# One core of an audio tower: the causal convolution on the 64-token blocks of one sequence alone, with the band matrices of two tiles packed into one, and a feed-forward whose up products are unsplit float32 and whose gelu output has two buffers

## The chip, the core and the metric

The kernel runs on one core of one Trainium2 chip. Its time is device microseconds (us). The engines are TensorE (PE, with its weight loads as PEld), VectorE (DVE), ScalarE (ACT), GpSimd (POOL) and SyncE (SP), which issues most transfers.

## The reference

Three layers work on 32 sequences of 64 tokens with 1024 features (2048 tokens).

```python
# 1. tokenizer
h = xf @ W_proj + b_proj                        # (32, 64, 1024)
y = _layernorm(h, ln_g, ln_b)
w = softmax((y @ W_wgen + b_wgen).reshape(B, 64, 8, 5), axis=-1)
yp = jnp.pad(y, ((0, 0), (4, 0), (0, 0)))
taps = jnp.stack([yp[:, k:k + 64] for k in range(5)], axis=0).reshape(5, B, 64, 8, 128)
conv = jnp.einsum('kbthr,bthk->bthr', taps, w).reshape(B, 64, 1024)
h = h + relu(conv @ W_ff + b_ff)
# 2. attention with 8 heads of 64 within each sequence
h = h + attn(_layernorm(h), w_qkv, w_o)
# 3. feed-forward of 16 heads, features permuted
t = _layernorm(h)[:, perm].reshape(-1, 16, 64)
t = gelu(jnp.einsum('bhd,hdm->bhm', t, up))     # 64 -> 256 per head
t = jnp.einsum('bhm,hmd->bhd', t, down)         # 256 -> 64 per head
h = h + t.reshape(-1, 1024)[:, unperm]
```

The convolution is causal with 5 taps, and its weights differ for every token and each of 8 heads of 128 features.

## The kernel before

The 2048 tokens are four chunks (`CH`) of `N` = 512, held as 8 blocks of 128 features by 512 tokens. A chunk has `TILES` = 4 tiles of 128 tokens, two sequences each. Every engine's order is written by hand, and counting semaphores are the only sync. The stages follow each other: input projection with the layernorm statistics and the logits (`a_step`, 0 to 211 us); the convolution of chunk 0 (211 to 229); W_ff of chunk c with the convolution of chunk c + 1 beside its last third (`b_step`, to 476); attention (`c_step`, to 808); output projection (`o_group`, to 909); feed-forward (to the end).

Large products are split in three: both operands are cut into a high part (ACT copy to float32r) and a low part (subtraction on DVE or POOL), and `split3` issues high·high, high·low, low·high. The statistics, the transposes, the convolution and the down products are unsplit float32, which the trace shows as two MATMUL records for each call (one for a transpose).

**The convolution as a product with a band matrix.** The softmaxed taps of a tile and head, 128 tokens by 5, are written to DRAM with a skew (`band_skew`) into a buffer that was filled with zeros before (`band_zero`, 2 x 1032 KB for each chunk), and read back as a 128 x 128 band (`band_load`, two transfers of 16 units for each chunk; 32 units are 4 tiles by 8 heads). For head h, `turn(n, h)` transposes the 4 tiles of y and the 4 bands, ACT copies the one (`turn_evac`), DVE the other (`band_evac`), `conv(n, h)` multiplies tile by tile with all 128 tokens contracted, and ACT and DVE make its high and low parts (`conv_high`, `conv_low`) for W_ff. y uses banks 0 and 1, the bands 2 and 3, the result 4 and 5, by turns.

**Weights.** `unit_load` brings units of 128 x 512 through a ring of four `stage` slots; ACT makes the high part (`unit_hi`), DVE or POOL the low one (`unit_lo`, L299), and a slot is loaded again when its low part is done. POOL starts the W_ff units when the last bands of chunk 0 are transposed (`at_mm` of 8). SP's queue has them behind the band loads of chunk 1, and `db_late`, whose mean `late_sum` forms on DVE (L1242) for PE's L319, behind 8 of those units.

**Feed-forward.** A step s is one pair of heads (a = s mod 8) of one chunk, 32 steps in all. `ff_up(s + 1)` fills banks 0 to 3 (two blocks of two row halves, 64 rows contracted; three passes), ACT applies gelu from the banks into `gt` (L1097), `ff_down(s)` multiplies `gt` by `dn_f` into bank 4 or 5 (L1838), DVE adds (`d_add`, L1442), POOL scatters (L763). PE's order is up(s + 1), down(s). Beside it, for the next chunk, POOL gathers (L757), DVE centres and scales (`d_prep`), ACT and DVE split (`xd_high`, `xd_low`). In steps 5 to 12 the variance of the last chunk is formed too: DVE centres a block (L383), ACT squares it (L387), POOL adds it (L341), and PE needs the sum after down(12) (`stat_var_pe`, L403).

## Time and profile before

| | |
|---|---|
| median of 3 runs | 1067.11 us (1065.8 to 1070.73) |
| the profiled execution | 1062.28 us, span 1060.5 us |
| PE, PEld, DVE, ACT, POOL busy | 92%, 70%, 50%, 42%, 38% |
| mean granted TensorE clock | 0.977 |
| DMA packets, MB | 71570, 133.15 |
| chain that ended last | PE 51%, issue 11%, POOL 8%, DVE 5% |
| PE busy in 211 to 275 us | 52.06 of 64.00, clock 0.92 |
| PE busy in 808 to 909.5 us | 88.80 of 101.50, clock 0.92 |
| PE busy in 909.5 to 1060.5 us | 123.4 of 151.0 |

Busy shares say how full an engine's row is; they don't say what a stretch waits for. For that the timeline is read: an engine, its line, what it writes and reads, and in brackets how long it idled before and for whom.

### The profile page before, as it was taken

To read this page: it belongs to the slowest core of one execution; us is meant where nothing else is said; L and a number is where in the kernel's file an instruction comes from. 1 tells how busy PE (TensorE), PEld (TensorE's weight loads), DVE (VectorE), ACT (ScalarE), POOL (GpSimd) and SP (SyncE) were. 2 spreads that over 40 slices of the span, in tenths; PEclk is the share of its full clock that TensorE was granted. 3 is DMA by queue.
4 is the path that set the end of the run, shared out by engine and by line. 5 is a ranking of instruction groups with operands and counts; after the bars stand their busy time and mean duration, and the time that the engine had idled before them with its cause. 6 is when DMAs were issued, how large, how long until landed. Compare 5 with 4: busy or idle time off the path is not lost.

```text
span 1060.5 us, 14600 instructions
## 1 busy us (share of the span) xinstructions
PE 975.1 (92%) x5532; PEld 746.9 (70%) x5532; DVE 534.4 (50%) x848; ACT 443.9 (42%) x757; POOL 400.2 (38%) x321
## 2 busy tenths in 40 slices
PE   7999999987999999999779999999999899788885
PEld 5877777775887988878567877877887677333332
DVE  6253535576457403353756255174064567976661
ACT  6244454544434433434243243242142332676663
POOL 1224343128502114622360450550023577757431
PEclk9999999998999999999989999999999998899999
DMA  8754653595353154327101202001217765634311
GB/s 292 272 199 25 218 39 144 41 339 187 112 172 106 60 149 173 112 96 248 41 11 37 74 11 72 39 12 38 73 58 235 225 218 199 193 115 137 132 60 60
DMA packets 71570, 133.15 MB, mean 126 GB/s; under 512 B 29255, under 2 KB 30279, under 8 KB 66894
## 3 DMA queue, kind: packets, MB, share of 16 engines
q1 hardware_dynamic: 65342, 115.29, 34.7%
q0 software_dynamic: 5120, 16.78, 4.7%
q8 instruction: 44, 0.72, 0.3%
q10 hardware_dynamic: 1040, 0.16, 0.1%
q14 instruction: 24, 0.20, 0.1%
HBM read 85.65 MB, written 46.56 MB: 125 GB/s over the span
## 4 chain that ended last, share of the span: by engine, by line
PE 51%; issue 11%; POOL 8%; DVE 5%; ACT 3%; DMA 3%; SPq 0%; POOLq 0%; ACTq 0%; DVEq 0%
PE bank L305 12%; PE bank L307 12%; PE bank L306 12%; PE bank L1828 4%; POOL vacc L341 3%; PE bank L1838 3%; PE bank L1583 2%; DVE sq L383 1%; ACT gt L1097 1%; DMA stage<-w_qkv_t 1%; POOL hg L757 1%; PE bank L1562 1%; DVE acc L1242 1%; POOL acc L314 1%; PE bank L1570 1%
## 5 line engine op out<-in xcount | busy, mean ns | idle before, releaser
L341 POOL TENSOR_TENSOR vacc<-vacc,sq 128x512 f32<-128x512 f32 x72 | 97.1, 1348 | 47.2 <-ACT sq L387 37.9
L305 PE MATMUL bank<-xa_h,wp_h 128*128 128x512 f32 x256 | 103.0, 402 | 7.2 <-DVE xa_l L1119 7.2
L305 PE MATMUL bank<-cv_h,wf_h 128*128 128x512 f32 x256 | 106.2, 415 | 3.2 <-POOL wf_l L299 3.2
L307 PE MATMUL bank<-cv_h,wf_l 128*128 128x512 f32 x256 | 101.7, 397 | 0.0
L306 PE MATMUL bank<-cv_l,wf_h 128*128 128x512 f32 x256 | 101.6, 397 | 0.0
L306 PE MATMUL bank<-xa_l,wp_h 128*128 128x512 f32 x256 | 100.7, 393 | 0.0
L307 PE MATMUL bank<-xa_h,wp_l 128*128 128x512 f32 x256 | 100.6, 393 | 0.0
L705 POOL TENSOR_TENSOR fo<-fo,res 128x512 f32<-128x512 f32 x32 | 43.7, 1379 | 129.8 <-ACT fo L844 92.8
L1097 ACT ACTIVATE gt<-bank 128x512 f32<-128x512 f32 x128 | 66.0, 601 | 20.2 <-PE bank L1838 20.0
L387 ACT ACTIVATE sq<-sq 128x512 f32<-128x512 f32 x56 | 35.0, 632 | 72.3 <-DVE sq L383 72.3
L1838 PE MATMUL bank<-gt,dn_f 128*64 128x512 f32 x256 | 62.5, 606 | 0.0
L305 PEld LDWEIGHTS bank<-xa_h,wp_h 128*128 128x128 f32 x256 | 48.7, 190 | 18.7 <-DVE xa_l L1119 7.2
L305 PE MATMUL bank<-xc_h,wq_h 128*128 128x512 f32 x128 | 54.7, 427 | 5.5 <-issue 5.5
L305 PEld LDWEIGHTS bank<-cv_h,wf_h 128*128 128x128 f32 x256 | 49.3, 193 | 14.3 <-issue 4.8
L763 POOL DMA_INDIRECT out<-hg,rows x32 | 37.4, 1169 | 54.4 <-DVE hg L1442 52.2
L305 PE MATMUL bank<-vs_h,wo_h 128*128 128x512 f32 x128 | 53.4, 417 | 4.6 <-DVE vs_l L1340 4.2
L307 PEld LDWEIGHTS bank<-cv_h,wf_l 128*128 128x128 f32 x256 | 49.1, 192 | 10.6
L306 PEld LDWEIGHTS bank<-cv_l,wf_h 128*128 128x128 f32 x256 | 49.2, 192 | 10.4 <-issue 1.2
L306 PEld LDWEIGHTS bank<-xa_l,wp_h 128*128 128x128 f32 x256 | 48.7, 190 | 10.6 <-issue 0.7
L307 PEld LDWEIGHTS bank<-xa_h,wp_l 128*128 128x128 f32 x256 | 48.6, 190 | 10.4
L1224 DVE COPY ar<-bank 128x512 f32<-128x512 f32 x32 | 22.1, 689 | 66.7 <-PE bank L1570 66.7
L305 PE MATMUL bank<-wv_h,xc_h 128*128 128x512 f32 x128 | 50.6, 396 | 2.2 <-DVE wv_l L299 2.2
(187 smaller groups left out, 2288.7 us busy)
## 6 DMA issues: line engine op xcount, KB each, us to landing
band_s<-zero SPq DMA_DIRECT2D x8, 1032.0 KB, 9.2
xs<-x_t SPq DMA_DIRECT2D x32, 256.0 KB, 6.3
h_s<-ho SPq DMA_DIRECT2D x8, 1024.0 KB, 6.7
res<-h_s SPq DMA_DIRECT2D x32, 256.0 KB, 3.2
h_s<-fo SPq DMA_DIRECT2D x32, 256.0 KB, 2.3
dc<-h_s SPq DMA_DIRECT2D x4, 2048.0 KB, 9.3
h<-h_s SPq DMA_DIRECT2D x8, 1024.0 KB, 8.4
h_s<-h SPq DMA_DIRECT2D x8, 1024.0 KB, 5.0
```

What stands on the lines that cost most here:

```text
L305: pe.matmul(o, wh, xh, start=start, stop=False)
L306: pe.matmul(o, wh, xl, start=False, stop=False)
L307: return pe.matmul(o, wl, xh, start=False, stop=stop)
L341: g.tensor_tensor(vacc[:, :], t[:, 0, :] if k == 1 else vacc[:, :], t[:, k % 2, :], ALU.add).then_inc(ln_pool, 1)
L387: act.activation(sq[:, k % 2, :], sq[:, k % 2, :], ACT.Square).then_inc(ln_sq, 1)
L705: g.tensor_tensor(fo[m % 4][:, :], fo[m % 4][:, :], res[:, m % 2, :], ALU.add).then_inc(ff_add, 1)
L763: g.indirect_dma_start(out=outs[c], out_offset=bass.IndirectOffsetOnAxis(ap=rows[:, k:k + 1], axis=0), in_=hg[:, hg_block(c) + k, :], in_o ...
L1097: act.activation(gt[:, i, :], bank[i][:, :], ACT.Gelu).then_inc(gelu_ok, 1)
L1224: v.tensor_copy(ar[:, h % 2, :], bank[AT_BANK + h % 2][:, :]).then_inc(ar_ev, 1)
L1583: mm = pe.matmul(bank[CV_BANK + h % 2][:, cols], yt[:, h % 2, cols], ar[:, h % 2, cols], start=True, stop=True)
L1828: mm = pe.matmul(bank[2 * blk + j][:, :], w[r, a, cols], x[r, a, :], start=n == 0, stop=n == len(passes) - 1)
L1838: pe.matmul(bank[4 + a % 2][side, :], dn_f[:, FFB * a + 2 * head + blk, :], gt[:, i, :], start=blk == 0, stop=blk == 1).then_inc(g_used, 1)
```

## The change

The convolution works on each sequence's block of 64 x 64. The band matrix of a unit keeps only 64 rows of the skewed buffer (row pitch 132 instead of 128, so that two sequences' 64 columns lie side by side in 128), and the bands of two tiles fill the two halves of the partitions. A chunk has 16 packed bands instead of 32: half the zeros, half the bytes and rows of `band_load` (in four transfers, not two), two band transposes for each head instead of four, and a copy on DVE of 256 columns, not 512. `conv` is 16 products of 64 x 64 x 64 in the four quarters of the array instead of 4 of 128; its result lies in two banks, one for each sequence of a tile, so `conv_high` and `conv_low` become two instructions of 256 columns each. Only chunk 0 has two pairs of banks; the others have banks 3 and 4 alone, and `conv(n, h)` waits for the low parts of head h - 1. In the feed-forward the up products become one unsplit float32 pass on `dd` and `up_f`; `xd_high`, `xd_low`, and the four units of `up` in the ring go, and `gt` gets a second buffer.

```diff
-BAND = P * (P + 1)
 UNITS = TILES * CONV_HEADS
+ROW = P + TAPS - 1
+BAND = SEQ * (ROW + 1) + SEQ
...
-        up_h = place("up_h", [P, KB, FF_MID], F32R, R1)
-        up_l = place("up_l", [P, KB, FF_MID], F32R, R1 + 8 * KIB)
+        up_f = place("up_f", [P, KB, FF_MID], F32, R1)
-        gt = place("gt", [P, FFB, N], F32, R2)
+        gt = [place(f"gt{i}", [P, FFB, N], F32, at) for i, at in enumerate((R2, R1 + 40 * KIB))]
...
+        def cv_out(n, h, s):
+
+            return bank[cv_banks(n, h)[s]][:, 0:N // 2].rearrange("p (t q) -> p t q", q=SEQ)
...
                 for i in range(2):
-                    part = slice(i * UNITS // 2, (i + 1) * UNITS // 2)
-                    sp.dma_start(dst[:, part, :], src[:, part, :]).then_inc(band_ld[n % 2][i], 16)
+                    part = slice(i * UNITS // 4, (i + 1) * UNITS // 4)
+                    for a in range(2):
+                        sp.dma_start(dst[a * SEQ:(a + 1) * SEQ, part, :], src[a][:, part, :])\
+                          .then_inc(band_ld[n % 2][i], 16)
...
-                act.activation(cv_h[:, h, :], bank[CV_BANK + h % 2][:, :], ACT.Copy).then_inc(cv_hi, 1)
+                for s in range(2):
+                    act.activation(one_seq(cv_h[:, h, :], s), cv_out(n, h, s), ACT.Copy).then_inc(cv_hi, 1)
...
-                    if 8 * c + a > 0:
-                        act.wait_ge(g_used, 4 * (8 * c + a - 1) + i + 1)
-                    act.activation(gt[:, i, :], bank[i][:, :], ACT.Gelu).then_inc(gelu_ok, 1)
+                    if 8 * c + a > 1:
+                        act.wait_ge(g_used, 4 * (8 * c + a - 2) + i + 1)
+                    act.activation(gt[a % 2][:, i, :], bank[i][:, :], ACT.Gelu).then_inc(gelu_ok, 1)
...
             def conv(n, h):
-                if h < 2:
-                    since(pe, ff_ev, n - 1, 8, 5 + h)
-                if h >= 2:
+                if n == 0:
                     since(pe, cv_lo, n, 8, h - 1)
+                elif h == 0:
+                    pe.wait_ge(ff_ev, 8 * (n - 1) + CV_BANKS[0][1] + 1)
+                else:
+                    pe.wait_ge(cv_lo, 8 * n + h)
                 since(pe, yt_ev, n, 8, h + 1)
                 since(pe, ar_ev, n, 8, h + 1)
+                halves = [slice(SEQ * i, SEQ * i + SEQ) for i in range(2)]
                 for t in range(TILES):
-                    cols = slice(t * P, (t + 1) * P)
-                    mm = pe.matmul(bank[CV_BANK + h % 2][:, cols], yt[:, h % 2, cols], ar[:, h % 2, cols],
-                                   start=True, stop=True)
+                    for f in range(2):
+                        col = t * P + f * SEQ
+                        for s in range(2):
+                            mm = pe.matmul(bank[cv_banks(n, h)[s]][halves[f], t * SEQ:(t + 1) * SEQ],
+                                           yt[halves[s], h % 2, col:col + SEQ],
+                                           ar[halves[s], h % 2, t * SEQ:(t + 1) * SEQ], start=True, stop=True)
...
-                passes = ((up_h, xd_h), (up_h, xd_l), (up_l, xd_h))
-                for n, (w, x) in enumerate(passes):
-                    for j, r in enumerate(halves):
-                        mm = pe.matmul(bank[2 * blk + j][:, :], w[r, a, cols], x[r, a, :],
-                                       start=n == 0, stop=n == len(passes) - 1)
+                for j, r in enumerate(halves):
+                    mm = pe.matmul(bank[2 * blk + j][:, :], up_f[r, a, cols], dd[r, a, :], start=True, stop=True)
...
-YT_BANK, AT_BANK, CV_BANK = 0, 2, 4
+YT_BANKS, AT_BANKS, CV_BANKS = (0, 2), (1, 5), ((3, 4), (6, 7))
...
+def cv_banks(n, h):
+
+    return CV_BANKS[h % 2 if n == 0 else 0]
```

On PE, beside the last third of W_ff of chunk 1, one head of chunk 2 stood like this (`db_next` is y, and the last row is the next head's):

```order
L1562 MATMUL bank<-ident,db_next 128x128 x4
L1570 MATMUL bank<-ident,band 128x128 x4
L1583 MATMUL bank<-ar,yt 128x128 x4
L305 MATMUL bank<-cv_h,wf_h 128x512
L306 MATMUL bank<-cv_l,wf_h 128x512
L307 MATMUL bank<-cv_h,wf_l 128x512
```

After the change the same head reads:

```order
L1523 MATMUL bank<-ident,db_next 128x128 x4
L1533 MATMUL bank<-ident,band 128x128 x2
L1551 MATMUL bank<-ar,yt 64x64 x16
L299 MATMUL bank<-cv_h,wf_h 128x512
L300 MATMUL bank<-cv_l,wf_h 128x512
L301 MATMUL bank<-cv_h,wf_l 128x512
```

The order is kept; two transposes are gone and 4 convolution calls became 16 small ones.

On PE at the end of the feed-forward, one step stood as:

```order
L1828 MATMUL bank<-xd_h,up_h 128x512 x2
L1828 MATMUL bank<-xd_l,up_h 128x512 x2
L1828 MATMUL bank<-xd_h,up_l 128x512 x2
L1828 MATMUL bank<-xd_h,up_h 128x512 x2
L1828 MATMUL bank<-xd_l,up_h 128x512 x2
L1828 MATMUL bank<-xd_h,up_l 128x512 x2
L1838 MATMUL bank<-gt,dn_f 64x512 x4
```

And now two steps of it read (the number behind `gt` is the buffer):

```order
L1795 MATMUL bank<-dd,up_f 128x512 x4
L1804 MATMUL bank<-gt_132,dn_f 64x512 x4
L1795 MATMUL bank<-dd,up_f 128x512 x4
L1804 MATMUL bank<-gt_131,dn_f 64x512 x4
L1795 MATMUL bank<-dd,up_f 128x512 x4
```

Twelve up calls became four, and down reads the two buffers by turns.

On SP's queue around the band loads of chunks 0 and 1 (`band_86` is chunk 0's) there stood:

```order
L505 DMA band_86<-band_s 128x16x128 x2
L463 DMA h_s<-ho 128x2048 x2
L474 DMA db_next<-h_s 128x4096
L480 DMA mt<-stat_s 128x512
L481 DMA rt<-stat_s 128x512
L505 DMA band<-band_s 128x16x128 x2
L277 DMA stage<-w_ff 128x512 x8
L474 DMA db_late<-h_s 128x4096
```

and now there stands:

```order
L498 DMA band_86<-band_s 64x8x128 x4
L454 DMA h_s<-ho 128x2048 x2
L465 DMA db_next<-h_s 128x4096
L471 DMA mt<-stat_s 128x512
L472 DMA rt<-stat_s 128x512
L498 DMA band<-band_s 64x8x128 x4
L274 DMA stage<-w_ff 128x512 x8
L465 DMA db_late<-h_s 128x4096
```

The places are the same; each chunk's band load has half the rows.

## Rows read from the trace of the kernel before

**Rows 1.** Timeline of PE, two feed-forward steps: start us, us, engine, line, what, [idle]

```profile
994.67 0.50 PE L1828 MATMUL bank<-xd_h,up_h 64*128 64x512 f32 x2 [0.46 <-ACT gt L1097]
...
998.86 0.50 PE L1828 MATMUL bank<-xd_h,up_h 64*128 64x512 f32 x2 [0.46 <-ACT gt L1097]
...
1000.08 0.39 PE L1828 MATMUL bank<-xd_l,up_h 64*128 64x512 f32 x2
1000.31 0.40 PE L1828 MATMUL bank<-xd_h,up_l 64*128 64x512 f32 x2
1000.64 1.94 PE L1838 MATMUL bank<-gt,dn_f 128*64 128x512 f32 x8
```

**Rows 2.** Timeline of PE, a down group with float32 work right behind it

```profile
918.65 1.94 PE L1838 MATMUL bank<-gt,dn_f 128*64 128x512 f32 x8
920.52 1.12 PE L391 MATMUL bank<-acc,mean_w 128*128 128x512 f32 x2
```

**Rows 3.** Timeline of all engines in one of steps 5 to 12

```profile
961.47 0.50 PE L1828 MATMUL bank<-xd_h,up_h 64*128 64x512 f32 x2 [0.78 <-ACT gt L1097]
...
965.26 0.69 DVE L1442 TENSOR_TENSOR hg<-bank,hg 128x512 f32<-128x512 f32 x1 [1.07 <-PE bank L1838]
...
965.96 0.50 PE L1828 MATMUL bank<-xd_h,up_h 64*128 64x512 f32 x2 [0.78 <-ACT gt L1097]
...
969.24 2.04 ACT L1097 ACTIVATE gt<-bank 128x512 f32<-128x512 f32 x4
969.42 1.26 POOL L341 TENSOR_TENSOR vacc<-vacc,sq 128x512 f32<-128x512 f32 x1 [0.50 <-ACT sq L387]
```

**Rows 4.** Timeline of all engines, one head of chunk 3's convolution beside W_ff

```profile
409.39 0.60 PE L1570 MATMUL bank<-ident,band 128*128 128x128 f32 x4
...
409.82 1.06 PE L1583 MATMUL bank<-ar,yt 128*128 128x128 f32 x8
...
410.64 0.47 PE L305 MATMUL bank<-cv_h,wf_h 128*128 128x512 f32 x1
410.92 0.60 ACT L839 ACTIVATE cv_h<-bank 128x512 fp32r<-128x512 f32 x1 [0.73 <-PE bank L1583]
...
411.55 0.69 DVE L1228 TENSOR_TENSOR cv_l<-bank,cv_h 128x512 fp32r<-128x512 f32 x1 [0.83 <-ACT cv_h L839]
...
412.97 0.50 PE L1583 MATMUL bank<-ar,yt 128*128 128x128 f32 x3
```

**Rows 5.** Timeline of all engines at a product of the attention in 64 x 64 pieces

```profile
807.90 0.69 PE L1735 MATMUL bank<-pt,vv 64*64 64x64 f32 x32
808.52 0.50 PE L305 MATMUL bank<-vs_h,wo_h 128*128 128x512 f32 x1
808.66 0.84 ACT L994 ACTIVATE vo<-bank,vec 128x256 f32<-128x256 f32 x2 [4.65 <-PE bank L1735]
```

**Rows 6.** Timelines of PE, SP, ACT and DVE between 211 and 265 us

```profile
214.17 0.66 PE L1570 MATMUL bank<-ident,band 128*128 128x128 f32 x4 [1.73 <-DMA band<-band_s]
...
218.06 11.55 SPq L505 DMA_DIRECT2D band<-band_s  x2
...
237.39 2.47 ACT L293 ACTIVATE wf_h<-stage 128x512 fp32r<-128x512 f32 x4 [7.86 <-DMA stage<-w_ff]
...
240.23 0.59 PE L305 MATMUL bank<-cv_h,wf_h 128*128 128x512 f32 x1 [3.16 <-POOL wf_l L299]
...
254.38 0.69 DVE L1242 TENSOR_TENSOR acc<-db_late 128x512 f32<-128x512 f32 x1 [8.68 <-DMA db_late<-h_s]
...
264.34 2.08 PE L319 MATMUL bank<-acc,mean_w 128*128 128x512 f32 x2 [5.91 <-DVE acc L1242]
```

**Rows 7.** Windows: PE, PEld, DVE, ACT, POOL busy, clock, DMA share, GB/s

```profile
220.00:225.00 5.00, 5.00 (x48) 5.00 (x47) 3.57 (x6) 3.24 (x6) 0.00 (x0) 1.00 1.04 437
```

**Rows 8.** Timelines of POOL and PE in the output projection

```profile
850.26 6.89 POOL L299 TENSOR_TENSOR up_l<-stage,up_h 128x512 fp32r<-128x512 f32 x4 [3.00 <-ACT up_h L293]
...
875.99 2.00 PE L403 MATMUL bank<-mean_w,vacc 128*128 128x1 f32 x8 [3.03 <-DVE h L1377]
```

More of the change, by code:

```diff
@@ L433, in band_zero @@
                 sp.wait_ge(zero_ok, 1)
-                half = UNITS * BAND // 2
-                for i in range(2):
-                    sp.dma_start(band_s[c, i * half:(i + 1) * half].rearrange("(p n) -> p n", p=P),
-                                 zero[:, :]).then_inc(band_zeroed[c], 16)
+                sp.dma_start(band_s[c].rearrange("(p n) -> p n", p=P), zero[:, :]).then_inc(band_zeroed[c], 16)
             band_zero(0)
@@ L610, in _ @@
                     if c + 1 == CH and m == 0:
-                        for u in range(U_O + 4, U_UP):
+                        for u in range(U_O + 4, U_END):
                             unit_load(sp, u)
@@ L738, in _ @@
             g.wait_ge(v_mm, 4 * CH)
-            for u in range(U_O, U_UP):
+            for u in range(U_O, U_END):
                 unit_lo(g, u)
@@ L775, in _ @@
                 o_sum(c)
-                if c == 1:
-                    for u in range(U_UP, U_END):
-                        unit_lo(g, u)
             gather(1)
@@ L834, in turn_evac @@
                 since(act, cv_mm, n, 8, h - 1)
-                act.activation(yt[:, h % 2, :], bank[YT_BANK + h % 2][:, :], ACT.Copy).then_inc(yt_ev, 1)
+                act.activation(yt[:, h % 2, :], bank[YT_BANKS[h % 2]][:, :], ACT.Copy).then_inc(yt_ev, 1)
             def conv_high(n, h):
                 since(act, cv_mm, n, 8, h + 1)
-                act.activation(cv_h[:, h, :], bank[CV_BANK + h % 2][:, :], ACT.Copy).then_inc(cv_hi, 1)
+                for s in range(2):
+                    act.activation(one_seq(cv_h[:, h, :], s), cv_out(n, h, s), ACT.Copy).then_inc(cv_hi, 1)
             def ff_relu(c, m):
@@ L1047, in c_step @@
                 if not ahead:
-                    for u in range(U_O + 4, U_UP):
+                    for u in range(U_O + 4, U_END):
                         unit_hi(act, u)
@@ L1060, in _ @@
             c_step(CH - 1, False)
-            def xd_high(n, k):
-                since(act, xd_sc, n, 8, k + 1)
-                since(act, up_mm, n - 1, 32, 4 * k + 4)
-                act.activation(xd_h[:, k, :], dd[:, k, :], ACT.Copy).then_inc(xd_hi, 1)
             for c in range(CH):
@@ L1077, in _ @@
                     vs_high(c + 1, range(PAIRS - 1))
-                else:
-                    for half in range(2):
-                        act.wait_ge(o_st[0][half], 16 * (CH // 2))
-                    xd_high(0, 0)
-                    xd_high(0, 1)
                 if c > 0:
@@ L1086, in _ @@
                     vs_high(c + 1, [PAIRS - 1])
-                if c == 1:
-                    for u in range(U_UP, U_END):
-                        unit_hi(act, u)
             def gelus(c, a):
@@ L1173, in gates @@
                 since(v, lgt_mm, n, 1, 1)
-                since(v, skewed, n - 1, 16, 16)
+                since(v, skewed, n - 1, 32, 32)
                 per = [P, UNITS, TAPS]
@@ L1223, in band_evac @@
                 since(v, cv_mm, n, 8, h - 1)
-                v.tensor_copy(ar[:, h % 2, :], bank[AT_BANK + h % 2][:, :]).then_inc(ar_ev, 1)
+                v.tensor_copy(ar[:, h % 2, :], bank[AT_BANKS[h % 2]][:, 0:N // 2]).then_inc(ar_ev, 1)
             def conv_low(n, h):
-                since(v, cv_hi, n, 8, h + 1)
-                v.tensor_tensor(cv_l[:, h, :], bank[CV_BANK + h % 2][:, :],
-                                cv_h[:, h, :].bitcast(F32), ALU.subtract).then_inc(cv_lo, 1)
+                for s in range(2):
+                    v.wait_ge(cv_hi, 16 * n + 2 * h + s + 1)
+                    ins = v.tensor_tensor(one_seq(cv_l[:, h, :], s), cv_out(n, h, s),
+                                          one_seq(cv_h[:, h, :].bitcast(F32), s), ALU.subtract)
+                ins.then_inc(cv_lo, 1)
             for h in range(CONV_HEADS + 1):
@@ L1450, in _ @@
                     d_prep(n + 1, [k])
[L1451 to L1456 removed]
+                d_prep(0, LAST_PREP.get(s, ()))
                 if s == 0:
@@ L1565, in turn @@
                 if h % 4 == 0:
-                    pe.wait_ge(band_ld[n % 2][h // 4], 16 * (n // 2 + 1))
+                    pe.wait_ge(band_ld[n % 2][h // 4], 32 * (n // 2 + 1))
                 if h >= 2:
-                    since(pe, ar_ev, n, 8, h - 1)
-                for t in range(TILES):
-                    mm = pe.transpose(bank[AT_BANK + h % 2][:, t * P:(t + 1) * P], b[:, h * TILES + t, :],
+                    pe.wait_ge(ar_ev, 8 * n + h - 1)
+                elif n > 0:
+                    pe.wait_ge(ff_ev, 8 * (n - 1) + AT_BANKS[h] + 1)
+                for u in range(TILES // 2):
+                    mm = pe.transpose(bank[AT_BANKS[h % 2]][:, u * P:(u + 1) * P], b[:, h * TILES // 2 + u, :],
                                       ident[:, :])
```

92 lines of the change are left out of this document (30 added, 62 removed).

## The prediction, made before the change was run

> **What bounds the kernel now.** I read the page first: PE is busy 92% of the span and holds 51% of the chain, so a stretch can become shorter in two ways, by less PE work where PE is full, or by a shorter wait where it idles. The list of waits says where it idles, and the timeline says why. Three stretches matter.
>
> The feed-forward is a round trip, not a full engine. A step takes 998.86 - 994.67 = 4.19 us, and PE idles 0.46 us in front of each for a gelu [rows 1]. With one `gt`, gelu(s + 1) may overwrite block i only after down(s) has read it, and up(s + 2) needs the bank that gelu(s + 1) empties; the reader is to see that up, down and gelu pass the turn around. In steps 5 to 12 a step takes 965.96 - 961.47 = 4.49 us, since the square stands between two gelu groups on ACT [rows 3].
>
> The convolution beside W_ff is full: a head takes 412.97 - 409.82 = 3.15 us with no idle on PE, and 0.82 us of it is `conv`, 0.43 the four band transposes [rows 4].
>
> Between 211 and 265 us PE waits for transfers and what follows from them: 1.73 us for chunk 0's bands, 3.16 for a W_ff low part, 5.91 for the late mean [rows 6]. The transfer engines are full there [rows 7], and SP holds its queue 11.55 us for chunk 1's two band loads before the first W_ff unit is issued [rows 6].
>
> **The change part by part.**
>
> *Feed-forward, steps without statistics (24).* Up is now four float32 calls of 512 columns in two pairs, where three float32r passes of two blocks stood. Down has four float32 calls of 512 columns in two pairs too; it holds PE from 918.65 to 920.52, 1.87 us, the change of shape behind it included [rows 2]. The trace shows no float32 pair of row halves with 128 columns. From below its cost is that of down, if the two halves overlap as the float32r halves do (both calls of a pass stand in one row of 0.40 us and the passes follow at 0.23 us [rows 1]); from above it is twice that, if they don't. I take 1.87, since the attention's 64 x 64 float32 pieces, which use both row halves, plainly overlap: 16 calls in 0.62 us [rows 5]. PE's work in a step is then 2 x 1.87 = 3.74 us. With two buffers gelu(s + 1) needs only up(s + 1); a gelu group is 2.07 us or less [rows 3] and `xd_high` is gone, so ACT hides in 3.74. DVE loses `xd_low`. The step becomes 3.74, full of PE: 0.45 x 24 = 10.8 us. If this cover were gone (ACT's 2.04 us in line with up, as now), the step would stay at 4.19.
>
> *Steps 5 to 12 (8).* Here the square stays in ACT's order between gelu(s) and gelu(s + 1), and it waits for DVE's centre, behind `d_add` of down(s - 1). From that `d_add` to the next gelu it is 969.24 - 965.26 = 3.98 us [rows 3]; `xd_low` takes 0.6 of it away. PE can now run up and down in the shadow of it in one step, but every second step up waits about 1 us for the late gelu. Worked through, two steps take 8.3 us, 4.15 each. POOL sets a floor: 4.49 - 0.50 idle = 3.99 us [rows 3]. 0.34 x 8 = 2.7 us. The last step's gelu no longer waits for down(30), and the two reloads of ACT's table behind L403 are hidden by two buffers: I take 0.8 us. Feed-forward together: -14.3 us (bounds -20 with no cost for a change of shape and steps 5 to 12 at POOL's floor, 0 if the round trip stays).
>
> *Heads beside W_ff (24).* Two transposes fewer: -0.22 us [rows 4]. `conv` is 0.82 us before. The attention's product has the same 16 calls on the same quarters of the array and takes 808.52 - 807.90 = 0.62 us [rows 5]; I add the 0.10 us that a change of shape costs (down starts 0.33 us behind the last up pass, whose passes follow at 0.23 [rows 1]). So -0.10, and -0.29 for a head with a little lost behind it: -7.0 us. The new wait on `cv_lo` of the head before: ACT begins 0.28 us after the 0.82 of `conv` [rows 4], so 0.90 us after the new start; its two copies take 0.84 [rows 5]; DVE's second half ends by about 2.25 us. The next `conv` comes at 2.86 us. The wait is hidden with 0.6 us to spare; behind it on PE stands the whole of W_ff. Bounds: -0.40 to +0.3 for a head.
>
> At this place the Trainium skill speaks against the change. In "TensorE: Matmul & The Clock Gate", section "Wait — 56ns, not 53.3ns?", it holds that start-to-start never falls below about 25 ns however small the product is. By the page the 32 records would take 0.80 us, `conv` would gain nothing, and the sum would be 3 to 4 us worse. The trace disagrees: 32 records in 0.62 us are 19 ns each [rows 5].
>
> *Chunk 0's convolution and the W_ff ring.* The band transposes of chunk 0 start as soon as y is there: half the rows, so the 1.73 us go. The 8 heads gain 0.3 each (ACT's 0.5 + 0.84 per head still fits in 1.45): -2.4. PE and POOL's first low part are thus some 4 us earlier. SP's band loads of chunk 1 take half of 11.55 us, and the full transfer engines [rows 7] lose half of two chunks' bands, so the first ring unit, landed at 237.39 [rows 6], should land near 229. PE would then need it at 232.7 and find it: the idle of 3.16 us goes, with the slow restart behind it. But what counts is the next wait. `db_late` is loaded behind the ring, and the mean it feeds ends PE's idle of 5.91 us at 264.34 [rows 6]. It moves as the ring moves, and PE arrives earlier too and waits as long as before. I take -9.0 us at that point; bounds 0 (the ring does not move: then all PE gains go into the 5.91) and -10.
>
> *Output projection.* POOL loses 6.89 us of low parts ahead of chunk 2's variance, whose chain ends with PE idle 3.03 us at L403 [rows 8]. At most that can go; I take -2.5. The unsplit `up` loads and fewer zeros cost nothing: they lie in stretches where PE is full.
>
> **The sum.** -14.3 - 7.0 - 9.0 - 2.5 = -32.8 us. The profiled execution took 1062.3 us, so its like would take 1029.5; the median of the runs is 1067.1, 4.8 above it, which would give 1034.3. I put 1032 us.
>
> **The rivals.**
>
> *The round trip stays* (chance 0.12): PE's order or ACT's holds gelu back even with two buffers. For it speaks that steps 5 to 12 keep a chain through DVE. Then no gain of 14.3: 1046 us.
>
> *The single pair of result banks serialises the heads* (0.12): two half copies on each engine have fixed costs, and `conv` waits for `cv_lo`. Against it stand 0.6 us of slack. If it eats the gain: 1039 us; with 0.4 us of wait in each of 21 heads it would be 1047.
>
> *The ring does not move* (0.14): what holds `db_late` is the skewed write or the zeros, which stay in number, and PE's lead goes into the wait for the mean. 1041 us.
>
> *The row halves of unsplit float32 don't overlap* (0.08), the other side. Up takes 2 x 1.72 + 0.15 = 3.6 us, the step 3.6 + 1.87 = 5.5: 24 x 1.3 + 8 x 1.0 = +39 instead of -14.3, so 1032 + 53 = 1085 us. It decides from a step of 4.85 us on, an up group of 3.0: below it the 18.5 us of the other parts keep the kernel faster. Against it stands the 0.62 us of [rows 5].
>
> *As forecast* 0.49; *more than forecast* (both bounds met, under 1015) 0.05.
>
> **How the numbers follow.** The time is the likeliest case's, 1032 (its own range 1020 to 1043). The range takes in the three rivals with less gain, two of them together, and the lower bounds: 1013 to 1053; the serial halves lie outside. A measurement tells about 0.5% from no change here, 5.3 us. Faster by more: 0.89. Within: 0.03, if several rivals meet. Slower: 0.08.
>
> **What would show it.** Feed-forward steps of 3.7 us with no idle before up, near 4.15 in steps 5 to 12; float32 up pairs that start together; heads of 2.86 us; `conv` of 0.62 to 0.72; no idle at the fifth W_ff group; L319 near 255 us. An up group near 3.6 us, or PE idle for `cv_l` in front of `conv`, would make it wrong.

## The result, and the profile after

The changed kernel took 1033.76 us (median of 4 runs, 1031.12 to 1037.73) where the kernel before took 1066.96: the ratio is 0.9686, 95% interval 0.9642 to 0.973. Run again in a later series it took 1032.87 us, ratio 0.9703 (0.9676 to 0.973). The forecast was 1032 us. The sum came out, but two of its four terms did not: the largest was about right, the second largest was a good deal too big, and the smallest was less than half of what came. That the sum came out is in part luck: an error of 7 us at one place met errors the other way at two others (see the account below).

The page of the changed kernel, its profiled execution (1035.96 us, span 1034.2):

```profile
PE 967.4 (94%) x6108; PEld 714.5 (69%) x6108; DVE 509.2 (49%) x848; ACT 424.4 (41%) x753; POOL 394.3 (38%) x317
...
DMA packets 75062, 124.96 MB, mean 121 GB/s; under 512 B 29159, under 2 KB 38375, under 8 KB 70894
...
L1795 PE MATMUL bank<-dd,up_f 64*128 64x512 f32 x256 | 67.9, 651 | 5.6 <-ACT gt L1077 5.4
```

PE lost 7.7 us of work and some 19 us of idle time. The packets rose while the bytes fell; that comes back below.

**Feed-forward.** The timeline of PE, two plain steps, and then all engines in one of steps 5 to 12, as [rows 1, 3]:

```profile
988.83 1.99 PE L1795 MATMUL bank<-dd,up_f 64*128 64x512 f32 x8
990.75 1.94 PE L1804 MATMUL bank<-gt,dn_f 128*64 128x512 f32 x8
992.62 1.99 PE L1795 MATMUL bank<-dd,up_f 64*128 64x512 f32 x8
```

```profile
942.39 2.01 PE L1795 MATMUL bank<-dd,up_f 64*128 64x512 f32 x8
...
944.33 1.94 PE L1804 MATMUL bank<-gt,dn_f 128*64 128x512 f32 x8
944.38 0.68 DVE L377 TENSOR_TENSOR sq<-h,mean_t 128x512 f32<-128x512 f32 x1
945.10 0.63 ACT L381 ACTIVATE sq<-sq 128x512 f32<-128x512 f32 x1 [1.88 <-DVE sq L377]
945.63 2.04 ACT L1077 ACTIVATE gt<-bank 128x512 f32<-128x512 f32 x4
946.85 2.01 PE L1795 MATMUL bank<-dd,up_f 64*128 64x512 f32 x8 [0.58 <-ACT gt L1077]
```

The bracket before up is gone in the plain steps: 1.92 us of up and 1.87 of down make 3.79, no gap between them. In steps 5 to 12 the square still stands between two gelu groups and waits 1.88 us for the centre, and every second up waits.

**A head beside W_ff**, the timeline of PE for chunk 3, as [rows 4]:

```profile
401.06 0.69 PE L1551 MATMUL bank<-ar,yt 64*64 64x64 f32 x32
401.69 0.50 PE L299 MATMUL bank<-cv_h,wf_h 128*128 128x512 f32 x1
...
403.62 0.38 PE L1533 MATMUL bank<-ident,band 128*128 128x128 f32 x2
403.93 0.69 PE L1551 MATMUL bank<-ar,yt 64*64 64x64 f32 x32
```

A head takes 403.93 - 401.06 = 2.87 us, `conv` 0.63, the band transposes 403.93 - 403.62 = 0.31, and no head waits for `cv_l`.

**Between 211 and 262 us**, timelines of all engines, as [rows 6]:

```profile
215.17 9.52 SPq L498 DMA_DIRECT2D band<-band_s  x4
226.04 5.47 POOL L293 TENSOR_TENSOR wf_l<-stage,wf_h 128x512 fp32r<-128x512 f32 x4 [34.85 <-PE bank L1533]
227.34 15.10 SPq L274 DMA_DIRECT2D stage<-w_ff  x8
234.66 2.48 ACT L287 ACTIVATE wf_h<-stage 128x512 fp32r<-128x512 f32 x4 [6.38 <-DMA stage<-w_ff]
235.38 13.52 POOL L293 TENSOR_TENSOR wf_l<-stage,wf_h 128x512 fp32r<-128x512 f32 x8 [3.87 <-ACT wf_h L287]
237.12 0.47 PE L299 MATMUL bank<-cv_h,wf_h 128*128 128x512 f32 x1 [1.18 <-POOL wf_l L293]
...
251.25 0.69 DVE L1219 TENSOR_TENSOR acc<-db_late 128x512 f32<-128x512 f32 x1 [1.80 <-DMA db_late<-h_s]
261.20 2.08 PE L313 MATMUL bank<-acc,mean_w 128*128 128x512 f32 x2 [7.50 <-DVE acc L1219]
```

The wait for the W_ff low part shrank from 3.16 to 1.18 us, but the wait for the late mean (L313, the mean of the last chunk's block `db_late`) grew from 5.91 to 7.50 [rows 6]: of what PE won ahead of it, 1.6 us were lost there. In front of the late mean stands a wait of DVE for the transfer of `db_late`: 8.68 us before [rows 6], 1.80 now.

**Output projection.** Of PE's waits of 4.04 us for `vs_l` and 3.03 us for the second chunk's variance [rows 8] none is left. The first of them, in the timeline of PE of the kernel before:

```profile
847.96 0.77 PE L305 MATMUL bank<-vs_h,wo_h 128*128 128x512 f32 x1 [4.04 <-DVE vs_l L1340]
```

The timelines of SP, first of the kernel before, then of the changed one, point at the cause, which `up_16` below tests:

```profile
822.90 11.33 SPq L274 DMA_DIRECT2D stage<-up  x16
...
835.52 1.00 SPq L581 DMA_DIRECT2D vs<-vals_s  x1
```

```profile
809.91 1.68 SPq L617 DMA_DIRECT2D up_f<-up  x2
...
812.90 1.04 SPq L575 DMA_DIRECT2D vs<-vals_s  x1
```

The four units of `up` were 16 transfers, each of which held SP about 0.6 us, and the load of `vs` for the third chunk stood behind them. It is issued 22.6 us earlier now, 13 of which are the kernel's own lead at this place.

### The profile page after: what moved, and what is told of

Its sections match the earlier page's. It is cut to its first block, busy times and chain, and to the rows that moved or that the text cites. A ratio compares the mean times of both kernels' runs of the same rounds, so it can differ in the third digit from the quotient of the medians.

```text
span 1034.2 us, 15644 instructions
## 1 busy us (share of the span) xinstructions
PE 967.4 (94%) x6108; PEld 714.5 (69%) x6108; DVE 509.2 (49%) x848; ACT 424.4 (41%) x753; POOL 394.3 (38%) x317
## 4 chain that ended last, share of the span: by engine, by line
PE 53%; issue 10%; POOL 7%; DVE 5%; DMA 3%; ACT 2%; another core or an unknown queue 1%; POOLq 0%; SPq 0%; DVEq 0%; ACTq 0%
PE bank L299 14%; PE bank L301 13%; PE bank L300 13%; PE bank L1795 3%; PE bank L1804 3%; POOL vacc L335 2%; PE bank L1551 1%; POOL out L758 1%; POOL acc L363 1%; DVE sq L377 1%; DMA stage<-w_qkv_t 1%; POOL acc L308 1%; DVE acc L1219 1%; PE bank L1523 1%; DMA db_late<-h_s 1%
## 5 line engine op out<-in xcount | busy, mean ns | idle before, releaser
L335 POOL TENSOR_TENSOR vacc<-vacc,sq 128x512 f32<-128x512 f32 x72 | 97.2, 1350 | 45.8 <-ACT sq L381 36.4
L1795 PE MATMUL bank<-dd,up_f 64*128 64x512 f32 x256 | 67.9, 651 | 5.6 <-ACT gt L1077 5.4
L758 POOL DMA_INDIRECT out<-hg,rows x32 | 35.3, 1103 | 53.5 <-DVE hg L1408 51.4
L1795 PEld LDWEIGHTS bank<-dd,up_f 64*128 64x128 f32 x256 | 22.4, 194 | 47.9 <-issue 42.2
L1408 DVE TENSOR_TENSOR hg<-bank,hg 128x512 f32<-128x512 f32 x32 | 22.1, 690 | 66.2 <-PE bank L1804 60.1
```

Of the source, the lines that this page charges most:

```text
L335: g.tensor_tensor(vacc[:, :], t[:, 0, :] if k == 1 else vacc[:, :], t[:, k % 2, :], ALU.add).then_inc(ln_pool, 1)
L758: g.indirect_dma_start(out=outs[c], out_offset=bass.IndirectOffsetOnAxis(ap=rows[:, k:k + 1], axis=0), in_=hg[:, hg_block(c) + k, :], in_o ...
L1408: v.tensor_tensor(dst, bank[4 + a % 2][:, :], dst, ALU.add).then_inc(d_ev, 1)
L1795: mm = pe.matmul(bank[2 * blk + j][:, :], up_f[r, a, cols], dd[r, a, :], start=True, stop=True)
```

## The experiments

All times below stand against the kernel before, run on the same chip in the same series. One execution of each was profiled, so it was cut into places: the start of the first transpose of y (L1523; L1562 before), the late mean (L313), the first product with `wv_h`, the first product with `vs_h` that waits for `vo`, the last L397 of the output projection, and the end of the span. Each number is the difference of two such starts, in us.

| kernel | first turn at | to late mean | to wv | to vs | to last L397 | to the end | span |
|---|---|---|---|---|---|---|---|
| before | 211.81 | 52.53 | 212.17 | 327.06 | 103.97 | 152.96 | 1060.5 |
| ff_only | 212.23 | 53.25 | 212.22 | 327.07 | 97.16 | 141.37 | 1043.3 |
| before_up_8 | 212.33 | 52.92 | 213.04 | 327.09 | 100.73 | 154.29 | 1060.4 |
| conv_only | 211.48 | 50.33 | 207.06 | 325.29 | 101.43 | 154.51 | 1050.1 |
| changed | 213.39 | 47.81 | 204.89 | 324.38 | 96.44 | 147.29 | 1034.2 |
| changed, again | 213.75 | 48.14 | 206.72 | 325.13 | 95.95 | 141.21 | 1030.9 |
| up_16 | 213.86 | 51.42 | 204.84 | 326.20 | 99.68 | 141.40 | 1037.4 |
| one_gt | 211.84 | 52.46 | 205.57 | 325.69 | 95.96 | 156.08 | 1047.6 |
| bands_late | 215.22 | 47.12 | 204.81 | 325.98 | 95.60 | 143.07 | 1031.8 |
| square_early | 213.21 | 50.20 | 208.13 | 325.19 | 96.14 | 137.53 | 1030.4 |
| mean_14_sq | 213.18 | 50.70 | 206.55 | 325.58 | 95.87 | 137.52 | 1029.4 |
| all_three | 211.95 | 48.50 | 206.95 | 324.49 | 96.01 | 137.70 | 1025.6 |
| relu_first | 213.10 | 51.73 | 200.34 | 324.48 | 95.94 | 137.51 | 1023.1 |
| relu_bands | 211.45 | 49.42 | 199.47 | 324.12 | 95.97 | 137.57 | 1018.0 |

The table also says how far one execution can be read. Six executions (`conv_only`, changed, again, `up_16`, `one_gt`, `square_early`) share the code up to the late mean and took 47.81 to 52.46 us there; in `mean_14_sq`, `all_three`, `relu_first` and `relu_bands` the late mean stands two groups of W_ff later in PE's order, so their third and fourth columns are to be read as a sum; the output projection and the feed-forward agree within 0.5 us where the code is the same, but for the 147.29 and 143.07.

**Halves of the change.** `ff_only` takes the feed-forward hunks of the diff alone, `conv_only` the others.

> The kernel before with the feed-forward half of the change alone (unsplit up, two gelu buffers, up loaded by two transfers), the convolution as before. Theory A, by places of the changed trace: the output projection loses 7.5 us and the feed-forward 5.7, so 1067 - 13 = 1054 us, the waits of 4.04 and 3.03 us in the output projection are gone, a plain feed-forward step takes 3.79 us, and 211 to 476 us stands as before (5.91 at L319's place). Theory B, as predicted: feed-forward -14.3 and output projection -2.5 us, 1050 us, with the wait of 4.04 still there.

1045.98 us, ratio 0.9833 (0.9799 to 0.9867).

> The kernel before with the convolution half alone. Theory A, by places: -4.7 us up to the late mean, -7.3 beside W_ff, about -2 behind it: 1067 - 14 = 1053 us, and the two waits of 4.04 and 3.03 us in the output projection and a feed-forward step of 4.19 us stay. Theory B, as predicted (-9.0 and -7.0): 1051 us. If this kernel and the one with the feed-forward half together gain about 27 us and not 33, the halves don't help each other.

1051.97 us, ratio 0.9884 (0.9861 to 0.9907). The product of the two ratios is 0.972, near the 0.9686 and 0.9703 of the whole change, so the halves neither help nor hinder each other much. `ff_only` has theory A's rows: both waits of the output projection are gone (one of 1.23 us for `vs_l` is left), and a plain step takes 3.79 us. Its gain of 17.7 us is more than the 13 expected, since the stall in the changed kernel's profile had hidden 6 us of the feed-forward's part (see the control). In `conv_only` the wait for `vs_l` is 2.63 us instead of 4.04 and that for the variance 1.25 instead of 3.03, with `up` as before, which neither theory had.

**SP's queue.** In the changed kernel, `up` by heads:

```diff
-            for s in range(2):
-                sp.dma_start(up_f[FF_IN * s:FF_IN * (s + 1), :, :],
-                             up.rearrange("(a s) d m -> s d a m", s=2)[s]).then_inc(up_ld, 16)
+            for head in range(FF_HEADS):
+                a, s = divmod(head, 2)
+                sp.dma_start(up_f[FF_IN * s:FF_IN * (s + 1), a, :], up[head]).then_inc(up_ld, 16)
```

> The changed kernel with the same bytes of up loaded in 16 transfers of one head each instead of 2. Theory A (SP's queue: in the kernel before, 16 transfers of up held it 11.4 us, the next store and the load of the third chunk's vs stood behind them): the load of vs is issued about 9 us later, PE waits 2 to 4 us for vs_l in the output projection and up to 3 us for the second chunk's variance, 1034 + 5 = 1039 us (1036 to 1041). Theory B (as predicted, the low parts of up on POOL were what was late, and they are gone here too): 1034 us and no new wait.

1037.98 us, ratio 0.9755 (0.9734 to 0.9776), against 0.9703 for the same kernel with two transfers. Timelines of SP and PE:

```profile
814.76 10.92 SPq L618 DMA_DIRECT2D up_f<-up  x16
...
826.97 1.02 SPq L575 DMA_DIRECT2D vs<-vals_s  x1
...
838.92 0.76 PE L299 MATMUL bank<-vs_h,wo_h 128*128 128x512 f32 x1 [2.68 <-DVE vs_l L1317]
```

The wait for `vs_l` is back with no low part of `up` on POOL at all: it is the queue. The output projection takes 3.7 us more than in the control. The wait for the second chunk's variance did not come back (0.48 us): with the low parts on POOL gone it is gone too, as the prediction had it. The other way round, the kernel before with 8 transfers of `up`:

```diff
-                for i in range(2):
-                    for s in range(2):
-                        e.dma_start(stage[64 * s:64 * s + 64, u % 4, i * FF_MID:(i + 1) * FF_MID],
-                                    up[4 * (u - U_UP) + 2 * i + s]).then_inc(stage_ld[u % 4], 16)
+                for s in range(2):
+                    dst = stage[64 * s:64 * s + 64, u % 4, :].rearrange("p (a m) -> p a m", a=2)
+                    four = up[4 * (u - U_UP):4 * (u - U_UP) + 4].rearrange("(a s) d m -> s d a m", s=2)
+                    e.dma_start(dst, four[s]).then_inc(stage_ld[u % 4], 16)
```

> The kernel before with the four up units loaded by 8 transfers instead of 16, same bytes, nothing else changed. Theory A (SP's queue was late by the 16 issues of 0.60 to 0.64 us each): the load of the third chunk's vs is issued about 5 us earlier, PE's wait of 4.04 us falls to 0 to 1 us, the wait of 3.03 us for the second chunk's variance shrinks too, 1067 - 4 = 1063 us, ratio 0.996. Theory B (POOL's 6.89 us of low parts of up, as the prediction had it): no change in either wait, ratio 1.000.

1063.15 us, ratio 0.9992 (0.9974 to 1.0011). The rows follow theory A: the wait of 4.04 us is gone, that of 3.03 is 1.11, and the place is 3.2 us shorter; a new wait of 2.33 us for the mean took a part. The time does not: theory A's ratio of 0.996 lies outside the interval, and a gain of 3.2 us (0.997) just outside it too. In this execution the other places together are 3.1 us longer. So the queue is shown for the wait, but a gain of the whole kernel before from it is not. PE's timeline:

```profile
855.52 1.32 PE L391 MATMUL bank<-acc,mean_w 128*128 128x512 f32 x2 [2.33 <-DVE acc L1386]
...
875.00 2.00 PE L403 MATMUL bank<-mean_w,vacc 128*128 128x1 f32 x8 [1.11 <-DVE h L1377]
```

**The second gelu buffer.** The changed kernel with `gt[0]` alone and the wait on step s - 1.

> The changed kernel with one gelu buffer, as before. Theory A (round trip): from the start of down to the next up 2.40 us as in the kernel before, then up's 1.91, so a step of 4.3 us with PE idle 0.5 us before up; with 4.5 in steps 5 to 12: 24 x 0.5 + 8 x 0.3 = 14 us more, 1048 us. Theory B (the shorter up is what counts, not the buffer): a step of 3.8 us, 1034 us.

1049.76 us, ratio 0.9876 (0.9852 to 0.9899). PE's timeline:

```profile
1001.32 2.02 PE L1795 MATMUL bank<-dd,up_f 64*128 64x512 f32 x8 [0.46 <-ACT gt L1077]
...
1005.66 2.02 PE L1795 MATMUL bank<-dd,up_f 64*128 64x512 f32 x8 [0.46 <-ACT gt L1077]
```

A step is 4.34 us, longer than before the change (4.19): unsplit up takes PE 1.92 us where the three float32r passes took 1.78, from 998.86 to 1000.64 [rows 1]. With one buffer the new up alone lost 3 us (156.08 against 152.96 from the last L397 on; 2.2 against the mean of the three executions with the old feed-forward); the second buffer is worth 14.9 us at this place (156.08 - 141.21). Two buffers with the split up of before were not tried.

**A control.**

> The changed kernel once more, unchanged, as a control. In the first profiled execution the feed-forward held a wait of 2.87 us for a gelu, behind which two groups ran at a lower clock, and the kernels of the first series that share its feed-forward needed 141.4 us from the last L397 of the output projection to the end, not 147.3. Theory A: that stall is of one execution, so 141.5 us here and no such wait. Theory B: it belongs to the changed kernel with the new convolution, and stands here too. From the first turn to L313 the same code took 47.8, 51.4 and 52.5 us: 47 to 53 is expected, and tells how far one execution can be read there.

1032.87 us; from the last L397 to the end 141.21 us and no stall. The 6 us belong to one execution (see the last section).

**The late mean.** `bands_late` moves one call in SP's order:

```diff
             b_load(1)
-            band_load(1)
...
                 res_load(c, 1)
+                if c == 0:
+                    band_load(1)
```

> The changed kernel with the band load of chunk 1 put behind all units of W_ff, the late block and the first two res loads in SP's queue. Theory A (the 512-byte packets of the bands share the transfer engines with the first units, which land 7.3 us after their issue at 227.3): the units land about 4 us after their issue, POOL's low parts and the load of the late block come 4 to 5 us earlier, L313 stands at 43 to 46 us from the first turn (47.8 to 52.5 before), the time falls by 4 us, ratio to before 0.965. Theory B (VectorE, which works on y of chunk 1 until 249.4 at half its speed beside POOL, sets the late mean): 2 us at most.

1031.92 us, ratio 0.9697 (0.967 to 0.9724), the same as the control. DVE's timeline, and the same place in the control:

```profile
232.02 1.99 DVE L1127 TENSOR_TENSOR db_next<-db_next,mt 128x512 f32<-128x512 f32 x2 [1.43 <-DMA rt<-stat_s]
233.93 1.78 DVE L1131 SCALAR_TENSOR_TENSOR db_next<-db_next,vec,rt 128x512 f32<-128x512 f32 x1
...
252.38 1.78 DVE L1220 TENSOR_TENSOR acc<-db_late 128x512 f32<-128x512 f32 x1
254.20 8.09 DVE L1220 TENSOR_TENSOR acc<-acc,db_late 128x512 f32<-128x512 f32 x6
```

```profile
252.98 0.69 DVE L1219 TENSOR_TENSOR acc<-db_late 128x512 f32<-128x512 f32 x1 [0.20 <-DMA db_late<-h_s]
```

The first units of W_ff were ready earlier (232.75 us, though PE had started 1.8 us later). The first landed 3.5 us after its issue instead of 6.1 in the control and 7.2 in the changed kernel's first profile. In the nine profiled executions of this study that keep the band load ahead of the ring and the late mean at its old place, the first unit landed 0.4 to 0.7 us after the last band transfer. `db_late` landed 33.8 us after the first turn instead of 39.2 in the control.

Of that 2 us reached DVE and 1 us the late mean, and the median shows none of it, since another limit stood close behind: DVE works without a gap from 232.02, when `rt` has landed, to the end of the late sum at 262.3, and begins that sum 37.2 us after the first turn instead of 39.2. So there are two limits. In the eleven profiled executions with the band load in its old place DVE waited 0.20 to 8.68 us for `db_late` and began the late sum within 0.04 us of its landing. In the three with the band load behind the units it did not wait, and its own y of chunk 1 was what came last. In `bands_late` an operation on y takes 1.78 us while POOL makes low parts, and 0.68 to 0.74 where it doesn't. The Trainium skill has the rule in "SBUF — State Buffer", section "Who interferes with whom": a DVE instruction with two SBUF inputs contends with a GpSimd instruction that reads SBUF, and the contention is an exclusive lock. The trace agrees: DVE's operations start 1.70 us apart, and the changed kernel's low parts on POOL 13.52 / 8 = 1.69 us.

**The centre ahead of the add.** In DVE's order of a feed-forward step:

```diff
                 c, a = divmod(s, KB)
+                if 0 <= s - STAT_FROM < KB:
+                    o_center(CH - 1, [s - STAT_FROM])
                 if s > 0:
                     d_add((s - 1) // KB, (s - 1) % KB)
...
-                if 0 <= s - STAT_FROM < KB:
-                    o_center(CH - 1, [s - STAT_FROM])
```

> The changed kernel with VectorE's centre of the last chunk put ahead of the add of the step before, in steps 5 to 12, so that ScalarE's square waits for nothing between two gelu groups. Theory A (the chain through VectorE and the square is what makes these steps 4.18 us, not POOL): steps of 3.8 to 4.0 us, POOL's own 4.0 us being next, -1.5 to -3 us. Theory B: POOL's chain of add, scatter and gather already sets the pace: 4.18 as now, no gain.

1030.54 us, ratio 0.9672 (0.9644 to 0.9699): not told from the control by the median time, but plain in PE's rows. Steps 5 to 12 take 3.79 us too, and the stretch to the end takes 137.53 us instead of 141.2.

```profile
937.65 1.99 PE L1795 MATMUL bank<-dd,up_f 64*128 64x512 f32 x8
...
941.43 1.99 PE L1795 MATMUL bank<-dd,up_f 64*128 64x512 f32 x8
```

POOL's three operations take about 4.0 us a step here (its adds start 4.00 to 4.24 us apart), as I had worked out, but that is no floor for PE: POOL falls behind by some 0.3 us a step and catches up later, since nothing on PE needs it before step 13.

**Following the chain of the late mean.** `mean_14_sq` adds to that kernel one edit, `if c == 0 and i == 12` to `i == 14` in front of `ln_mean_pe`; `all_three` adds `bands_late` as well.

> The changed kernel with the early centre in steps 5 to 12 and the matrix product of the late mean (L313) put two groups of W_ff later. Theory A: VectorE forms the late sum by about 261 whatever PE does, so PE, two groups (4.1 us) further when it asks, waits 2 to 4 us at L313 instead of 6.2 to 8.2; behind it the centre of 4.9 us now ends about 1 to 2 us after PE is through with the last two groups, so 2 to 3 us are gained. Feed-forward 137.5 us from the last L397 as with the early centre alone. 1030.5 - 2.5 = 1028 us, ratio to before 0.965. Theory B: the wait only moves to the third group (for the centre), nothing gained, 1030.5 us.

1031.57 us, ratio 0.9699 (0.9675 to 0.9724). Timelines of PE and ACT:

```profile
263.88 1.13 PE L313 MATMUL bank<-acc,mean_w 128*128 128x512 f32 x2 [2.86 <-DVE acc L1219]
...
275.59 0.63 ACT L324 ACTIVATE sq<-db_late 128x512 f32<-128x512 f32 x1 [0.78 <-POOL vacc L335]
276.12 1.83 ACT L837 ACTIVATE fo<-bank,vec 128x512 f32<-128x512 f32 x3
...
278.00 0.69 PE L1533 MATMUL bank<-ident,band 128*128 128x128 f32 x2 [5.94 <-ACT fo L837]
```

The idle time at L313 fell by half (6.17 us in the control), and 14 us later a wait that was 1.96 us in the control is 5.94. Theory B had the size right, but not the wait: it is for neither the centre nor y. ACT has the eight squares of the late chunk, one for each of POOL's adds, in front of the relus that empty the bank of the second band transpose.

> The same with the band load of chunk 1 behind the units of W_ff as well. Theory A (the late sum hangs on VectorE's y of chunk 1, slowed beside POOL, not on the ring): no more than 1 us beside the kernel without it, 1027 to 1029 us. Theory B (the ring's earlier units do help once PE asks later): 2 us or more.

1030.04 us, ratio 0.9674 (0.9657 to 0.969). Then ACT's order was changed, so that only two squares stand ahead of the relus:

```diff
-                    for k in range(KB):
+                    for k in range(2):
                         ln_square_act(act, CH - 1, k, db_late[:, k, :])
...
                     if ahead and h > 0:
                         conv_high(c + 1, h - 1)
+                    if first and h < KB - 2:
+                        ln_square_act(act, CH - 1, h + 2, db_late[:, h + 2, :])
```

> The kernel with the early centre and the later mean product, and on ScalarE only two of the eight squares of the late chunk ahead of the relus of groups 3 to 5 of W_ff, the other six one by one behind the heads' copies. Theory A (the late mean's chain goes on through POOL's adds, 1.41 us for each square, and holds the relus that free the bank of the second band transpose; this is where the 3 us gained at L313 went): the wait of 5.94 us in front of that transpose falls under 1 us, from the first turn to wv 252 us instead of 257, 1031.6 - 5 = 1026.5 us, ratio to before 0.965. Theory B (another wait of the same chain, for the centre or for y of chunk 1, takes its place): the sum from the first turn to wv stays at 256 to 258, and the ratio at 0.970.

1024.74 us, ratio 0.9563 (0.9537 to 0.9588). The wait in front of that transpose is gone, and from the first turn to wv it takes 252.07 us instead of 257.25, as theory A had it. The time fell by 6.8 us (1031.57 to 1024.74); the ratio fell by more because the kernel before took 1070.66 us in this series and 1064.93 in that of `mean_14_sq`. The squares' move was not tried without the later mean product.

> The same with the band load of chunk 1 behind the units of W_ff. Theory A: the ring is no limit, so within 1.5 us of the kernel without it. Theory B: with VectorE's and ScalarE's chain out of the way the earlier ring counts, 2 us or more faster than the kernel without it.

1026.56 us, ratio 0.9583 (0.9555 to 0.961), the same within the intervals. The profiled execution, the fastest of its five, is 3.2 us shorter up to wv (248.89), so the runs show no gain from the ring and do not rule out one of a microsecond or two. `relu_first` is faster than both kernels of this case (0.9563 against 0.9703 for the changed one, each against the kernel before in its own series).

## Why the prediction was right in its sum and wrong in two of its terms

**Steps without statistics: as forecast.** 3.79 us against 3.74; up is 1.92 rather than 1.87, that is 0.40 us gained in a step, not 0.45. The row halves of unsplit float32 overlap (an up group is eight records of 0.65 us each in 1.92 us), so the rival of 1085 us is out, and `one_gt` shows what the round trip would have left. The 1.72 and 0.15 us from which that rival's group was added up stand in no row; twice the 1.87 of down would have given 3.7 instead of 3.6 us and changed nothing. **Steps 5 to 12**: 946.85 - 938.50, two steps, is 8.35 us, forecast 8.3. From the last L397 to the end the kernels with the old feed-forward took 153.9 us on average and those with the new one, the stalled execution left out, 141.8 (four of them): -12.2 where -14.3 was forecast. Of the missing 2 us, 1.2 are the 0.05 of each of 24 steps; the rest may be the ends, for which no row was looked up and whose 0.8 us the prediction took without one.

**Heads beside W_ff: right in sum.** 2.87 us against 2.86 (3.15 before), -6.7 us in 24; the places from the late mean to wv give -6.3. Two parts of it missed by 0.09 us or so, one each way: `conv` gave 0.19 us, where 0.10 was put, since the 0.10 added for a change of shape did not come, and the two transposes gave 0.12 us (0.43 to 0.31) where 0.22 was put. The wait on `cv_lo` is hidden, as worked out, so the rival of the single bank pair is out. `conv` is 0.63 us, as the row of the attention had it. The least distance of 25 ns between two starts that the Trainium skill gives in "TensorE: Matmul & The Clock Gate", section "Wait — 56ns, not 53.3ns?", would have made it 0.80 us, by an estimate from that figure for 32 records; the trace does not keep to it here.

**Chunk 0's convolution and the ring: this term failed.** It was put at -9.0 us. The places up to the late mean went from 52.9 (three kernels) to 50.1 (six), -2.8. With the heads it is 265.4 to 256.3, -9.1 us where -16.0 was forecast. What failed is how far the ring moves: the first unit was to land 8.4 us earlier (237.39 to 229), and counted from the first turn it landed 3.3 us earlier (26.6 in three executions, 23.4 in six). Three steps lead there.
- "The band transposes of chunk 0 start as soon as y is there: half the rows, so the 1.73 us go." PE still waited 1.8 to 2.4 us for the bands in five of the six new kernels. Half the rows are not half the time: the transfers of the packed bands go in packets of 512 bytes. The rise in packets under 2 KB is 9216 - 1024 = 8192, which is 4 chunks by 4 transfers by 64 x 8 rows; in the kernel before the same transfers came 2 KB at a time. The likely reason is that a row has a pitch of 132 now; no run varied the pitch alone. The DMA view at 211 to 214 us, chunk 0's bands, of the kernel before and of the changed one:

```profile
DMA packets 446, 0.89 MB, mean 296 GB/s; under 512 B 13, under 2 KB 13, under 8 KB 446
```

```profile
DMA packets 1417, 0.79 MB, mean 262 GB/s; under 512 B 46, under 2 KB 1406, under 8 KB 1406
```

  And at 226 to 229 us, chunk 1's bands, again before and changed:

```profile
DMA packets 513, 0.99 MB, mean 329 GB/s; under 512 B 38, under 2 KB 38, under 8 KB 512
```

```profile
DMA packets 1143, 0.61 MB, mean 202 GB/s; under 512 B 37, under 2 KB 1126, under 8 KB 1142
```

  With the engines full in all four, the small packets moved 262 and 202 GB/s, the large ones 296 and 329.
- "PE and POOL's first low part are thus some 4 us earlier." POOL's first low part ended 2.4 us earlier from the first turn. Beside the band wait, in three of the six (changed, `up_16`, `one_gt`) PE stood 1.2 us in front of a band transpose of chunk 0, which the profile gives to "issue"; that was not looked into.
- "SP's band loads of chunk 1 take half of 11.55 us." SP was held 9.52 us by four transfers. But the queue was not the only gate: the first unit's issue, 229.66 before, moved only to 227.34, because its slot is free when POOL has made its first low part (226.04 to 227.3), and POOL waits for the last band transpose of chunk 0. Then the unit landed only behind the packets of the bands, 7.2 us after its issue, where `bands_late` needed 3.5.

The next step, "it moves as the ring moves", held: `db_late` landed 2.7 us earlier from the first turn on average (43.3 to 40.6), DVE began the late sum as it landed in all nine of these executions, and the late mean came 2.8 us earlier. What the prediction did not see is the limit close behind. DVE's y of chunk 1 begins when `rt` has landed and is slowed beside POOL, and it held the late sum in `bands_late`, where the ring had moved further. And where PE asked later (`mean_14_sq`), the same chain, through centre, squares, POOL's adds and relus, gave the time back.

**Output projection: right that it gains, wrong how much, and one of two causes missed.** Forecast -2.5; the place went from 103.97 (101.43 in `conv_only`) to 95.6 to 97.2 in the kernels with two transfers of `up`, -4 to -8 us. The step that failed is "the unsplit `up` loads and fewer zeros cost nothing: they lie in stretches where PE is full": it looked at PE and not at what was queued behind 16 issues on SP. `up_16` puts 3.7 us of the gain down to them, in the wait for `vs_l`. The prediction's own cause, POOL's 6.89 us of low parts ahead of the wait of 3.03 us, is not refuted: with them gone that wait is 0.48 us in `up_16`, though the 16 issues stay. With them in place it is 1.11 in `before_up_8` and 1.25 in `conv_only`, so it hangs on more than the one. What the rest of the gain is due to was not tried apart.

**Not in the sum.** From wv to vs 327.1 became 325.3 us, in stalls that the profile gives to "issue"; the first turn came 1 us later. Neither was looked into.

By the places the terms are +0.8 (first turn), -9.1, -1.8, -6.6 and -12.2, together -28.9 us, which agrees with 1060.5 - 1030.9 = 29.6. The forecast of -32.8 was near by luck: 7 us too much for the ring and 2 for the feed-forward met 6 too little at two others, the output projection and the stretch ahead of it. The starting point helped too: the profiled execution of the kernel before was 4.8 us below the median of its runs, and 1032 was put between the two times that follow from them.

## What to carry to other kernels

When a wait is for a transfer, read the queue that issues it and count the issues ahead of it, not only their bytes: 16 issues of 0.6 us held back a load that PE needed, and two did not. When one wait goes, look up which engine's order holds the next one of the same chain; here the mean product was moved first and gave nothing, and only with the squares behind the relus did the time come out at the end. Look also for what stands just behind a wait that is to go: with the transfer of `db_late` 5.4 us earlier, DVE's own work let only 2 us through. And where three engines pass a turn around, look at the buffer before the length of any one's work: here a second one was worth 14.9 us, with a product that had even become longer.

## What the runs showed that I had not expected

In the changed kernel's first profiled execution ACT and DVE started 2 to 3 us after what they waited for. Timelines of PE, ACT and DVE, and then the same place in the control:

```profile
903.20 1.94 PE L1804 MATMUL bank<-gt,dn_f 128*64 128x512 f32 x8
904.01 0.60 ACT L370 ACTIVATE mean_t<-bank 128x512 f32<-128x512 f32 x1 [4.32 <-remote]
906.78 2.07 ACT L1077 ACTIVATE gt<-bank 128x512 f32<-128x512 f32 x4 [2.17 <-remote]
907.01 0.69 DVE L1408 TENSOR_TENSOR hg<-bank,hg 128x512 f32<-128x512 f32 x1 [3.81 <-remote]
908.01 2.93 PE L1795 MATMUL bank<-dd,up_f 64*128 64x512 f32 x8 [2.87 <-ACT gt L1077]
910.87 2.67 PE L1804 MATMUL bank<-gt,dn_f 128*64 128x512 f32 x8
```

```profile
903.17 1.13 PE L385 MATMUL bank<-acc,mean_w 128*128 128x512 f32 x2
...
904.41 0.60 ACT L370 ACTIVATE mean_t<-bank 128x512 f32<-128x512 f32 x1 [1.79 <-PE bank L385]
```

The releaser is "remote", that is, unknown: the mean of L385 was done on PE at about 901.3 (the next product starts at 901.29), ACT's copy came at 904.01, and DVE's add at 907.01 though down was done at 905.1. The control's copy came 0.2 us after the mean (903.17 + 1.06, where the next product starts). PE then idled 2.87 us and ran two groups at a lower clock, 6 us in all (147.29 against 141.21 to 141.40 at that place); the granted clock was 0.66 at 908 to 911 us and 0.77 at 911 to 914. The view by windows gives the transfer engines a share of 1.02 at 904 to 906 us (the busy times of PE, PEld, DVE, ACT and POOL, the clock, the share, GB/s):

```profile
904.00:906.00 2.00, 1.14 (x6) 0.14 (x2) 0.00 (x0) 0.60 (x1) 0.98 (x1) 1.00 1.02 387
```

Full transfer engines alone do not bring it about: in the control the share was 0.95 at 904 to 906 us and 1.01 at 906 to 908, without a stall. It stood in one of the fourteen profiled executions of this study, and nothing was tried to bring it about; whether the signal or its reader was late stays open.

The second finding is the price of a small packet with the engines full (262 and 202 GB/s in packets of 512 bytes, 296 and 329 in packets of 2 KB, one window of 3 us each), and the third that DVE's operations with two SBUF inputs lengthen from 0.68 us to 1.78 beside POOL, which sets the pace of a stretch that I had read as bound by transfers as soon as the transfers are earlier.
